# Moving tile 0's LoRA work, its loads and the last tile's half products in a fused conditional-matrix and LoRA kernel

## The reference

```
x = x + einsum('bct,bcd->bdt', x, W0[cond])           # a 32x32 matrix per sample, 16 to choose from
x = x + x @ W + b + 2 * (x @ A[id]) @ B[id]           # W 512x512; A 512x16, B 16x512 per sample, 32 to choose from
```

## Time and profile before

| | |
|---|---|
| median of 3 runs | 85.14 us (84.99 to 85.22) |
| the profiled execution, own time | 85.35 us |
| its span | 83.6 us |
| busy: PE, VectorE (DVE), ScalarE (ACT), GpSimd (POOL) | 79.6, 59.3, 52.0, 35.0 us |
| granted TensorE clock in the page | full in all 40 slices |

### The profile page before, as it was taken

How to read it: one execution, slowest core, us unless ns; L and a number is a source line. 1 busy time by engine, 2 the same in 40 slices (tenths; PEclk the granted TensorE clock), 3 DMA queues, 4 the chain that set the end, 5 groups by cost and what they waited for, 6 DMA issues and landing times.

```text
span 83.6 us, 1999 instructions
## 1 busy us (share of the span) xinstructions
PE 79.6 (95%) x521; PEld 71.8 (86%) x521; DVE 59.3 (71%) x154; ACT 52.0 (62%) x179; POOL 35.0 (42%) x75
## 2 busy tenths in 40 slices
PE   4999999999999999999999999999999999999970
PEld 2368688999899999999999999999999999999930
DVE  2048495885888787777878787888787777876540
ACT  1545757766566675958666666666685957669120
POOL 6128888844442617080715344342617080303000
PEclk9999999999999999999999999999999999999999
DMA  0999779899776768676586878676874734120333
GB/s 13 307 347 315 143 199 261 165 365 329 209 239 163 239 196 245 197 206 213 143 250 171 238 178 241 174 248 151 219 211 159 177 110 152 45 92 7 119 125 125
DMA packets 15997, 16.06 MB, mean 192 GB/s; under 512 B 10225, under 2 KB 10482, under 8 KB 15986
## 3 DMA queue, kind: packets, MB, share of 16 engines
q1 hardware_dynamic: 14016, 11.74, 47.4%
q0 software_dynamic: 1248, 4.06, 17.0%
q10 hardware_dynamic: 722, 0.14, 0.9%
HBM read 11.74 MB, written 4.19 MB: 191 GB/s over the span
## 4 chain that ended last, share of the span: by engine, by line
PE 85%; DMA 6%; ACTq 3%; ACT 2%; issue 1%; DVE 1%
PE z_ps L548 58%; PE z_ps L585 9%; DMA a_raw<-in_lora_a 6%; PE y_ps L596 4%; PE y_ps L600 4%; PE y_ps L598 4%; PE ht_ps L572 2%; ACTq L323 1%; PE z_ps L580 1%; PE ht_ps L626 1%; ACT L317 1%; PE y_last L608 1%; PE y_ps L608 1%; ACTq L313 1%; DVE y_sb L534 1%
## 5 line engine op out<-in xcount | busy, mean ns | idle before, releaser
L548 PE MATMUL z_ps<-wa,x_hi 128*128 128x288 f32 (+2 forms) x240 | 50.3, 301 | 0.0
L548 PEld LDWEIGHTS z_ps<-wa,x_hi 128*128 128x128 f32 x240 | 38.0, 188 | 1.8 <-issue 0.5
L548 PE MATMUL z_ps<-wa,x_lo 128*128 128x288 f32 (+2 forms) x120 | 35.5, 296 | 0.0
L548 PEld LDWEIGHTS z_ps<-wa,x_lo 128*128 128x128 f32 x120 | 22.6, 188 | 0.0
L291 POOL DMA_INDIRECT b_raw<-in_lora_b,b_index_slot x16 | 17.6, 1097 | 4.4 <-POOL b_index_slot L289 4.4
L300 POOL CAST m_hi<-m_raw 128x128 fp32r<-128x128 f32 x15 | 4.4, 293 | 31.5 <-ACT m_raw L337 31.5
L480 DVE TENSOR_TENSOR z_lo<-z_ps,z_hi 128x256 fp32r<-128x256 f32 x30 | 11.3, 420 | 6.4 <-ACT z_hi L381 6.4
L381 ACT CAST z_hi<-z_ps 128x256 fp32r<-128x256 f32 x30 | 9.7, 376 | 9.7 <-PE z_ps L585 9.6
L337 ACT COPY m_raw<-w_raw 32x32 f32 x64 | 13.8, 216 | 1.8 <-DVE w_raw L502 1.2
L439 DVE TENSOR_TENSOR x_lo<-x_raw,x_hi 128x512 fp32r<-128x512 f32 x14 | 9.7, 690 | 3.5 <-ACT x_hi L349 3.5
L460 DVE TENSOR_TENSOR b_lo<-b_raw,b_hi 128x512 fp32r<-128x512 f32 x15 | 10.4, 693 | 1.6 <-ACT b_hi L369 1.1
(11 more groups left out here) (51 smaller groups left out, 78.8 us busy)
## 6 DMA issues: line engine op xcount, KB each, us to landing
out<-y_sb SPq DMA_DIRECT2D x15, 256.0 KB, 2.4
x_raw<-in_xt SPq DMA_DIRECT2D x14, 256.0 KB, 2.9
a_raw<-in_lora_a SPq DMA_DIRECT2D x60, 32.0 KB
first_sb<-in_first SPq DMA_DIRECT2D x2, 384.0 KB, 4.0
first_sb<-in_first SPq DMA_DIRECT2D x3, 256.0 KB, 4.8
b_raw<-in_lora_b,b_index_slot POOLq DMA_INDIRECT x16, 4.0
bias_sb<-in_bias SPq DMA_DIRECT2D x1, 256.0 KB, 5.2
out<-y_sb SPq DMA_DIRECT2D x2, 128.0 KB, 1.7
```

Of the source, the lines that this page charges most:

```text
L548: done = nc.tensor.matmul(target, (x_lo if lo_x else x_hi)[s][:, k, :], moving(lo_w), start=first and not lo_x and not lo_w, stop=last and ...
```

## The change

It does these things:

- SyncE issues A of tile 0 after the first four pieces and before the fifth (x of tile 1); ScalarE issues A of tile 1. ScalarE makes tile 0's copy of A before it rounds x of tile 1.
- VectorE works out B's row indices, after two of the four additions of the identity to W.
- Tile 0's `lora` runs in fp32r like the others: B of tile 0 is gathered with all rows and split by ScalarE and VectorE, and its masked h is split by two more VectorE operations. It stands after 18 instead of 12 of tile 1's main products.
- GpSimd adds the identity to the small matrices, between the gathers of tile 1 and tile 2.
- From tile 2 on, a tile's first product waits for the first half of z of the tile two before, the second half of its products for the second.
- In the last tile `transpose_h` and `lora` of tile 14 stand earlier, `lora` of tile 15's first half too; the first half of the last M z is three fp32r matmuls, the second half two fp32 matmuls of 128 columns. Three parts are finished and stored, the last one by ScalarE's queue.

```diff
@@ sync
-            for n in range(len(PIECES) - 1):
+            for n in range(PIECE_OF_X1):
                 load_first(n)
             sp.wait_ge(ids_loaded, 16)
-            load_a(1)
+            load_a(0)
+            load_first(PIECE_OF_X1)
             load_x(2)
...
-            for half in range(2):
-                sp.wait_ge(y_ready, LAST + 1 + half)
+            for n, at in enumerate(PARTS[:-1]):
+                sp.wait_ge(y_ready, LAST + 1 + n)
...
@@ gpsimd
-            pool.wait_ge(ids_p_loaded, 16)
-            pool.tensor_copy(r_of_p[:, :], ids_p_sb[:, TILES:TILES + 1]).then_inc(r_ready, 1)
...
-            for u in range(NB):
-                gather_b(u)
-            for u in range(LAST):
+            gather_b(0)
+            gather_b(1)
+            pool.wait_ge(ident_ready, 1)
+            pool.wait_ge(w0_loaded, 16)
+            pool.tensor_tensor(w0_raw[:, :, :], w0_raw[:, :, :],
+                               ident[0:C, 0:C].rearrange("p (a d) -> p a d", a=1).broadcast_to([C, S0, C]),
+                               ALU.add).then_inc(w0_plus_i, 1)
+            gather_b(2)
+            for u in range(TILES):
                 split_m(u)
@@ scalar
-            round_x1(0)
             act.wait_ge(a_loaded[0], 16 * J)
             act.copy(a0_sb[:, :, :].rearrange("p k (j r) -> p k j r", j=J),
                      a_raw[0][:, :, :, :].rearrange("p j k r -> p k j r")).then_inc(a0_ready, 1)
+            round_x1(0)
             round_x1(1)
             round_a(1)
             round_w(KC - 1)
             round_x(2)
+            round_b(0)
             round_a(2)
...
+            act.wait_ge(lora_done, 2 * LAST + 2)
+            for n in range(2):
+                act.copy(z_sb[:, n * P:(n + 1) * P], z_of(LAST, 1)[:, n * P:(n + 1) * P]).then_inc(z_copied, 1)
+            act.wait_ge(y_ready, LAST + len(PARTS))
+            act.dma_start(out_rows[LAST * P:(LAST + 1) * P, PARTS[-1]],
+                          y_sb[LAST % 2][:, PARTS[-1]]).then_inc(last_part_stored, 16)
@@ vector
                     nc.vector.tensor_tensor(ht0_sb[:, :], ht_ps[0:JR, 0:P],
                                             own_mask0[:, :, :].rearrange("p j c -> p (j c)"),
-                                            ALU.mult).then_inc(ht_ready, 1)
+                                            ALU.mult).then_inc(ht0_step, 1)
+                    dve.wait_ge(ht0_step, 1)
+                    nc.vector.tensor_copy(ht_sb[0][0:JR, :], ht0_sb[:, :]).then_inc(ht0_step, 1)
+                    dve.wait_ge(ht0_step, 2)
+                    nc.vector.tensor_tensor(ht_sb[0][JR:P, :], ht0_sb[:, :], ht_sb[0][0:JR, :],
+                                            ALU.subtract).then_inc(ht_ready, 1)
...
             mask_ht(0)
-            dve.wait_ge(w0_loaded, 16)
-            nc.vector.tensor_tensor(w0_raw[:, :, :], w0_raw[:, :, :],
...
+            rest_b(0)
             rest_x(2)
@@ tensor
             def wait_main(u):
...
-                    pe.wait_ge(z_ready, 2 * (u - 1))
+                    pe.wait_ge(z_ready, 2 * (u - 1) - 1)
...
-            def mix_last(half):
+            def mix_last_half():
...
+            def mix_last_quarter(n):
```

More of the change, by code:

```diff
@@ L412, in _ @@
             build_m(LAST - 1)
-            build_m(LAST)
-            round_h(LAST)
             for half in range(2):
                 round_z(LAST - 1, half)
-            for half in range(2):
-                act.wait_ge(lora_done, 2 * LAST + half + 1)
-                act.copy(z_sb[:, cols(half)], z_of(LAST, half)).then_inc(z_copied, 1)
+            round_h(LAST)
+            build_m(LAST)
+            round_z(LAST, 0)
+            act.wait_ge(lora_done, 2 * LAST + 2)
[4 more added lines that the diff above has]
+                          y_sb[LAST % 2][:, PARTS[-1]]).then_inc(last_part_stored, 16)
         @block.vector
@@ L488, in finish_y, with index_b @@
                                         ALU.add).then_inc(y_ready, 1)
+            def index_b():
+                dve.wait_ge(ids_p_loaded, 16)
+                nc.vector.tensor_copy(r_of_p[:, :], ids_p_sb[:, TILES:TILES + 1]).then_inc(r_ready, 1)
+                dve.wait_ge(r_ready, 1)
+                nc.vector.tensor_scalar(b_index[:, :], ids_p_sb[:, 0:TILES], float(R), r_of_p[:, 0:1],
+                                        ALU.mult, ALU.add).then_inc(b_index_ready, 1)
             dve.wait_ge(ident_ready, 1)
             add_identity(0)
-            for k in range(KC - 1):
+            add_identity(1)
+            index_b()
+            rest_w(0)
+            for k in range(1, KC - 1):
                 add_identity(k + 1)
@@ L522, in _ @@
             rest_h(LAST - 1)
+            mask_ht(LAST - 1)
             rest_b(LAST)
-            mask_ht(LAST - 1)
             finish_y(LAST - 2)
-            rest_h(LAST)
             rest_z(LAST - 1, 0)
             rest_z(LAST - 1, 1)
+            rest_h(LAST)
             mask_ht(LAST)
             finish_y(LAST - 1)
+            rest_z(LAST, 0)
             dve.wait_ge(y_stored[LAST % 2], 16 * (LAST // 2))
-            for half in range(2):
-                dve.wait_ge(y_computed, LAST + 1 + half)
-                nc.vector.tensor_tensor(y_sb[LAST % 2][:, cols(half)], (y_ps[LAST % 2], y_last)[half][:, cols(half)],
-                                        bias_sb[:, cols(half)], ALU.add).then_inc(y_ready, 1)
+            for n, at in enumerate(PARTS):
+                dve.wait_ge(y_computed, LAST + 1 + n)
+                nc.vector.tensor_tensor(y_sb[LAST % 2][:, at], y_part(n), bias_sb[:, at], ALU.add).then_inc(y_ready, 1)
         @block.tensor
@@ L560, in main_chunk @@
                     pe.wait_ge(a_ready, 2)
+                elif k == 0 and half == 1:
+                    pe.wait_ge(z_ready, 2 * (u - 1))
                 return products(u, k, z_ps[s][:, half, 0:NW],
@@ L577, in lora @@
                 pe.wait_ge(ht_ready, u + 1)
[L578 to L583 removed]
+                pe.wait_ge(b_ready, u + 1)
                 for b_part in (b_hi, b_lo):
@@ L647, in last_chunk @@
             def last_chunk(k, half):
+                if k == 0 and half == 1:
+                    pe.wait_ge(z_ready, 2 * (LAST - 1))
                 n = (HALF + 2 * AC, HALF)[half]
```

90 lines of the change are left out of this document (47 added, 43 removed).

## The result

The changed kernel takes 86.58 us (median of 4 runs, 86.23 to 86.92) where the kernel before took 85.18 beside it (84.99 to 85.26): a ratio of 1.0154 (95% interval 1.0128 to 1.0180), **1.3 us slower** by the ratio. The profiled execution took 86.51 us, 1.16 more than the one of before; its span is 84.5 us, 0.9 more, and the rest lies outside the span: own time less span is 2.0 where it was 1.75.

A forecast was written before the change was run, and what follows sets the result against it. PE, busy 95% of the span, was taken as the bound, with only tiles 0 to 3 and the tail counting: 85.35 - 0.25 - 0.3 = 84.8 us for the profiled execution, 84.6 for the median; range 83.8 to 85.5.

The forecast's parts named there:

- A of tile 0 on SyncE's queue: Load order at the start: x of tile 1 0.7 us later, yet tile 1's main products 0.2 earlier.
- T1: Start of tile 1's main products on PE: forecast 10.45, bounds 0.35 us earlier to 0.25 later.
- Tile 0's LoRA in fp32r: Tile 0's LoRA, behind 18 main products of tile 1: 0.85 us saved on PE.
- T2: Start of tile 2's main products on PE: 0.6 us earlier, bounds 1.0 earlier to 0.3 later.
- Its list had room, I charge 0.2: VectorE ahead of z of tile 0: some 0.6 us more work, charged as 0.2 us.
- The identity on GpSimd: Addition to the small matrices ahead of the third gather: 1.3 us on GpSimd, hidden for ScalarE, which waits for it.
- rival 3: Slower: GpSimd's addition holds VectorE 1.3 us, then B of tile 2 lands at 20.35; 85.7 us (85.4 to 86.4), chance 0.16.
- B of tile 2: Its gather lands at 19.2, holding tile 2's LoRA, so only 0.25 us of 0.73 is left.
- rival 2: B of tile 2 lands at 19.45 to 19.85 and swallows the early gain; 84.85 to 85.25 us, no change, chance 0.22.
- The tail: Last tile's new end, from the last LoRA product to the last addition: 0.3 us gained, bounds 0 and 0.5.

The follow-up runs named there:

- e6: The kernel before with the swap of the two load queues alone (A of tile 0 on SyncE, A of tile 1 on ScalarE): 85.86 us, ratio 1.0046.
- e15: e8 with the mask of the later tiles cleared and filled by GpSimd instead of VectorE: 84.64 us, ratio 0.9936.
- e3: The changed kernel with two parts undone, loads in their old queues and the identity added on VectorE: 85.68 us, ratio 1.0032.
- e9: The kernel before with tile 0's LoRA in fp32r alone, addition, index operations, queues and end as before: 85.69 us, ratio 1.0062.
- e4: The kernel before with only the identity added on GpSimd, between the gathers of tiles 1 and 2: 85.66 us, ratio 1.0027.
- e2: The changed kernel with the load queues as before, the addition still on GpSimd: 85.71 us, ratio 1.0048.
- e8: The changed kernel with queues as before, small matrices loaded ahead of x of tile 1, GpSimd's addition between gathers of tiles 0 and 1: 84.85 us, ratio 0.9941.
- e5: The kernel before with the new end of the last tile alone: 84.94 us, ratio 0.9973.
- e13: The kernel before with 8 more VectorE instructions at the start, each clearing one unread column: 85.78 us, ratio 1.0045.
- e14: The kernel before with z awaited by halves alone: 85.09 us, ratio 0.9985.
- e7: The changed kernel with x of tile 1 issued ahead of A of tile 0 in SyncE's list only: 86.77 us, ratio 1.0139.

## Why the prediction was wrong

**A of tile 0 on SyncE's queue: sized wrongly.** "I take x 0.7 us later, 8.9" counted the bytes ahead of x; the upper end of the bounds, T1 0.25 later, did so too, and so did the 0.3 at which the prediction took the swap to be inside its cases. x came at 9.83 and T1 0.72 later, for the step did not count the instructions: four issues at 0.48 and the wait for the list ahead of them. The row for it was in the trace of before. And the gain of it was nil: A came at 9.05 for 9.14. Alone the swap costs 0.39 us (e6), and in a third of the executions of the kernels that have it the mean clock was 0.98 besides.

**Tile 0's LoRA in fp32r: right, but it takes all the room there is.** LoRA itself took 0.55 us (14.77 to 15.32), and where nothing is late T2 - T1 is 3.87 (e15), as forecast (10.48 to 14.35). "Its list had room, I charge 0.2" holds for the list that the change makes. But how much room was left for anything else was not looked up. These rows of the kernel before show it, ScalarE, then VectorE:

```profile
12.92 0.90 ACT L337 COPY m_raw<-w_raw 32x32 f32 x4 [1.23 <-DVE w_raw L502]
13.85 0.65 ACT L381 CAST z_hi<-z_ps 128x256 fp32r<-128x256 f32 x2
...
14.25 0.76 DVE L480 TENSOR_TENSOR z_lo<-z_ps,z_hi 128x256 fp32r<-128x256 f32 x2 [0.97 <-ACT z_hi L381]
```

VectorE idled 0.97 us ahead of z, of which 0.85 was to be saved. The list grows by 0.7 (masks from 13.05 to 13.94, one of 0.2 before; B 0.6; less the addition of 0.6), which fits in e15 with z awaited by halves (there the second half of z ended at 14.69, after T2). It grows by 1.3 where the addition stays (e3, e9), and work ahead of the addition finds no room in that gap at all, since z stood right behind M, and M waited for the addition. So LoRA in fp32r alone is a loss of 0.53.

**The identity on GpSimd: duration right (1.35 for 1.3), "hidden" wrong.** This step made T2 - T1 5.15 where 3.87 was to be had. It is the first half of rival 3, to which 0.16 was given: the addition came at 11.02, between VectorE's subtractions, and VectorE stood. The argument against it, that VectorE's time had not grown in the rows of before, drew on rows in which VectorE had started first. By the Trainium skill (SBUF — State Buffer, "SBUF: two separate sides") the two engines share a port pair as an exclusive lock. The trace now agrees in the direction that was missing: the pair of 0.49 took 1.59 beside the addition's 1.35 and 1.57 beside 1.34, and a subtraction of 0.67 took 1.58 beside 1.41. It costs only 0.23 alone (e4), as VectorE gives away 0.67 of its own and had room, so that T2 waited for M and not for VectorE's list; with LoRA in the list nothing of that room was left, and it costs 1.15 (e2 against e8).

**B of tile 2: the wait that was to decide did not occur.** The rounding at 19.90 has no idle time, though its gather was issued later (12.84 for 11.80). It lies in the window that the prediction set (18.5 to 20), but by chance: ScalarE came there so late by itself, and whether B landed at 19.2 can't be read from it. The step, and with it rival 2 and the second half of rival 3, built on one execution's late landing (7.6 us from the issue). e5, e6, e13 and e14 keep that gather and rounded B of tile 2 at 18.40 to 19.22 without a wait; e5 and e14 waited for B of tile 1 instead (0.49, 0.55).

**The tail: right.** 0.28 in the profile, 0.23 alone (e5).

**Left out: the time outside the span.** The prediction took 1.75 us as given; the changed kernel has 1.97.

In the profiled executions the account closes: T1 0.72 later, T2 - T1 0.52 longer and 0.25 more outside the span, less 0.28 in the tail, make 1.2 us; measured were 1.16. By the ratio it is 1.31 (1.09 to 1.53). Two of the four executions of the changed kernel (86.64, 86.92) had a mean clock of 0.98; the two at 1.0 (86.51, 86.23) lie 1.19 above the median of before, so the clock may be the rest, which four executions can't settle. Even rival 3 (85.4 to 86.4), nearest to 86.58, had neither x so late nor the time outside the span.

The six parts alone add up to 0.87 us (0.39 + 0.23 + 0.53 + 0.08 - 0.23 - 0.13), with the 0.22 outside, which only all of them together bring, to 1.09. That this comes near is in part luck, since the parts act on each other: the 0.53 of e9 has the addition in VectorE's list, which the change takes out, and the hold that costs 0.23 in e4 costs 1.15 where LoRA fills the list.

## What to carry to other kernels

Before work is added to an engine's list, add up that list between the two points for which another engine waits, set it against the idle gap in front of the end, and look at what ends that gap. Here the gap had 0.97 us; work that saves TensorE 0.85 and makes the list 0.7 longer just fitted (e15), and whatever came on top, a hold of 1.1 or an addition of 0.6 for which M waits, was lost time. A GpSimd operation that touches SBUF belongs into a gap of VectorE's list, and a transfer that is moved behind others is late by the issues ahead of it, not by their bytes. Make room at the early end, as with the small matrices here, and the same fp32r LoRA that cost 0.53 us is part of a kernel 0.54 us faster.

## What was not expected of the hardware

- VectorE's subtraction stood while GpSimd's addition on SBUF, which had started first, ran: 0.28 us of work took 1.38 beside an addition of 1.35.
- Own time outside the span goes up with the number of VectorE's instructions: 1.75 us from 153 to 157, about 1.96 at 160, about 2.08 at 161 and 162. Eight idle clearings at the start, which delay nobody, cost 0.34 us.
- After gaps of 1.53 and 1.15 us TensorE's granted clock was 0.50 for 3 us (e7); 18 products took 1.3 us longer, and executions of e7 at a mean clock of 0.98 took 1.04 us more than those at 1.0. In the profiled execution of the changed kernel, with gaps of 0.53 and 0.74, it stayed at 1.0, but two of its four executions had 0.98, as had 9 of 27 of the kernels with A of tile 0 on SyncE's queue and none of the others.
